# Embedding interactions with a small network on one core: one comparison per chunk, shorter VectorE subtractions, pair loads right behind stores

## What is computed

```python
e = jnp.stack([tbl_0[ids[:, 0]], ..., tbl_25[ids[:, 25]]], axis=1)
combined = jnp.concatenate([dense_features[:, None, :], sparse_features], axis=1)
interactions = jnp.einsum('bfd,bgd->bfg', combined, combined)
interactions_flat = interactions[:, _IU0, _IU1]
z = jnp.concatenate([dense_features, interactions_flat], axis=1)
h = jnp.concatenate([z, r_dense_features], axis=1)
h = jnp.maximum(h @ W_top1 + b_top1, 0.0)     # 607 x 512
h = jnp.maximum(h @ W_top2 + b_top2, 0.0)     # 512 x 256
y = h @ W_top3
```

## Time and profile before

| | |
|---|---|
| Time, median of 3 runs | 526.63 us (525.46 to 535.25) |
| The profiled execution's own time | 522.24 us |
| Its span | 520.4 us |
| TensorE, busy | 373.9 us (72%) |
| GpSimd, busy | 352.1 us (68%) |
| VectorE, busy | 257.9 us (50%) |
| ScalarE, busy | 205.5 us (39%) |
| TensorE's granted clock, mean | 0.852 of full speed |
| DMA queues, share of 16 engines | 34.3% (SP's), 12.6% (the gathers) |

### The profile page before, as it was taken

How to read it: one execution, slowest core, us unless ns; L and a number is a source line. 1 busy time by engine, 2 the same in 40 slices (tenths; PEclk the granted TensorE clock), 3 DMA queues, 4 the chain that set the end, 5 groups by cost and what they waited for, 6 DMA issues and landing times.

```text
span 520.4 us, 8177 instructions
## 1 busy us (share of the span) xinstructions
PE 373.9 (72%) x3360; PEld 299.5 (58%) x3360; DVE 257.9 (50%) x186; ACT 205.5 (39%) x278; POOL 352.1 (68%) x266
## 2 busy tenths in 40 slices
PE   0969689496908450899975782889981937669997
PEld 0758477475807340778854471678851726456887
DVE  5778689483965105659760535649760001102123
ACT  2996945424623123153622425154530314225500
POOL 7888888887888775868887676868887570730000
PEclk9988989797968775799997795799995866779999
DMA  8975746961763513358357353358331520114320
GB/s 197 250 180 153 198 114 182 295 176 42 193 161 108 147 50 90 86 153 210 99 144 193 91 134 95 86 136 219 102 84 50 150 67 6 51 32 108 73 65 10
DMA packets 40327, 64.85 MB, mean 125 GB/s; under 512 B 22013, under 2 KB 22909, under 8 KB 40292
## 3 DMA queue, kind: packets, MB, share of 16 engines
q1 hardware_dynamic: 31152, 47.14, 34.3%
q0 software_dynamic: 8192, 16.79, 12.6%
q10 hardware_dynamic: 948, 0.41, 0.3%
HBM read 54.08 MB, written 10.23 MB: 124 GB/s over the span
## 4 chain that ended last, share of the span: by engine, by line
PE 38%; POOL 24%; issue 15%; another core or an unknown queue 12%; DVE 9%; DMA 1%; ACT 1%; DVEq 0%; ACTq 0%
POOL rows L571 24%; PE look_bank L610 12%; PE short_bank L693 9%; PE out_bank L640 7%; DVE one_hot L901 5%; PE out_bank L654 4%; PE out_bank L649 3%; PE short_bank L678 3%; DVE low_table L888 2%; PE out_bank L666 1%; DMA rows<-in_tbl,all_ids 1%; DVE low_pairs L946 1%; DMA all_ids<-in_ids 0%; DVE low_dense L946 0%
## 5 line engine op out<-in xcount | busy, mean ns | idle before, releaser
L571 POOL DMA_INDIRECT rows<-in_tbl,all_ids x256 | 351.1, 1371 | 109.4 <-issue 75.7
L901 DVE TENSOR_TENSOR one_hot<-spread_ids,chunk_row 128x2048 fp32r<-128x2048 int32 (+2 forms) x82 | 171.2, 2123 | 49.2 <-PE look_bank L610 22.3
L610 PE MATMUL look_bank<-one_hot,high_table 125*128 125x512 f32 x328 | 148.5, 453 | 22.3 <-DVE low_table L888 12.0
L610 PE MATMUL look_bank<-one_hot,low_table 125*128 125x512 f32 x328 | 139.4, 425 | 4.5 <-issue 4.5
L914 DVE COPY all_combined<-short_bank 128x512 f32<-128x512 f32 x32 | 21.7, 690 | 163.9 <-PE short_bank L678 73.3
L610 PEld LDWEIGHTS look_bank<-one_hot,high_table 125*128 125x128 f32 x328 | 69.4, 212 | 44.3 <-DVE low_table L888 12.0
L693 PE MATMUL short_bank<-all_combined 128*59 128x54 f32 x2048 | 71.5, 228 | 23.9 <-issue 22.3
L693 PEld LDWEIGHTS short_bank<-all_combined 128*59 128x59 f32 x2048 | 65.8, 142 | 34.5 <-issue 33.8
L610 PEld LDWEIGHTS look_bank<-one_hot,low_table 125*128 125x128 f32 x328 | 69.1, 211 | 21.8 <-issue 7.5
L678 PE MATMUL short_bank<-identity,rows 128*128 128x128 f32 x256 | 40.0, 303 | 57.8 <-issue 30.1
L678 PEld LDWEIGHTS short_bank<-identity,rows 128*128 128x128 f32 x256 | 31.2, 154 | 63.1 <-issue 57.2
(11 more groups left out here) (41 smaller groups left out, 200.8 us busy)
## 6 DMA issues: line engine op xcount, KB each, us to landing
whole_table<-in_tbl SPq DMA_DIRECT2D x36, 448.0 KB
spread_ids<-in_ids_by_feature SPq DMA_DIRECT2D x40, 256.0 KB
block_scratch<-all_dots SPq DMA_DIRECT2D x24, 208.0 KB
rows<-in_tbl,all_ids POOLq DMA_INDIRECT x256
block_scratch<-all_dots SPq DMA_DIRECT2D x24, 104.0 KB
whole_table<-in_tbl SPq DMA_DIRECT2D x4, 560.0 KB
pairs<-block_scratch SPq DMA_DIRECT2D x72, 29.2 KB
whole_table<-in_tbl SPq DMA_DIRECT2D x36, 52.0 KB
```

The lines of the kernel that those rows point to most:

```text
L571: nc.gpsimd.indirect_dma_start(rows[:, t % 2, slot, :], None, tables[ROW_FEATURES[slot]][:, :], bass.IndirectOffsetOnAxis(ap=all_ids[:, t, ...
L610: last = nc.tensor.matmul(look_bank[s % LOOK_BANKS][:], table_parts[part][s % TABLE_PLACES][0:ROWS_K, c, :], one_hot[0:ROWS_K, (chunks_bef ...
L901: last = nc.vector.tensor_tensor(one_hot[:, place:place + n, :], spread_ids[:, s % ID_PLACES:s % ID_PLACES + 1, :].to_broadcast([P, n, COLS]),
```

## The change

Three edits. (1) VectorE makes the one-hots with one comparison of 512 columns per chunk; and the low parts of tables (in two instructions, of 512 or 640 columns), pairs and weights (one instruction per slice of 512) are subtracted in shorter instructions. Since the lists of views are shared, ScalarE's casts of pairs and weights are cut in the same way; its casts of tables aren't. (2) At a block's end SP issues the pair loads right behind the stores, ahead of the first look's ids and table instead of behind them. (3) Behind a block's four tiles stand 4, 6, 7 and 7 products of the block before instead of 6 each. No sum and no number type changes.

```diff
--- before.py
+++ after.py
@@ -78,6 +78,8 @@
 
 HALVES_AFTER = [6, 5, 5, 4]
 
+OUTS_AFTER = [4, 6, 7, 7]
+
 FIRST_MOVES = [(0, 8), (8, N_LOOK)]
 
 PART_PAIRS = [(HIGH, HIGH), (HIGH, LOW), (LOW, HIGH)]
@@ -169,7 +171,7 @@
                 half[4:-1] + one[:2] + half[-1:] + one[2:-1] + two[:2] + one[-1:] + two[2:]][u]
     first = (m + 1) * 2 * N_LOOK + sum(HALVES_AFTER[:u])
     looks = [step for half in range(first, first + HALVES_AFTER[u]) for step in look_steps(half)]
-    outs = out_steps(m - 1)[6 * u:6 * u + 6] if m > 0 else []
+    outs = out_steps(m - 1)[sum(OUTS_AFTER[:u]):sum(OUTS_AFTER[:u + 1])] if m > 0 else []
     if u == 0:
 
         return looks[:2 * SPLIT_BESIDE] + merge(looks[2 * SPLIT_BESIDE:], outs, 1.0)
@@ -417,12 +419,12 @@
 
         def weight_parts(w):
 
-            return w[:, 0, :], w[0:K_PAIRS, 1:K_TILES, :]
+            return [w[:, 0, :]] + [w[0:K_PAIRS, k, :] for k in range(1, K_TILES)]
 
         def input_views(m):
 
             return [(dense_cols[:, m % 2, :], high_dense[:], low_dense[:, m % 2, :]),
-                    (pairs[0:K_PAIRS], high_pairs[0:K_PAIRS], low_pairs[0:K_PAIRS])]
+                    *[(pairs[0:K_PAIRS, k], high_pairs[0:K_PAIRS, k], low_pairs[0:K_PAIRS, k]) for k in range(PAIR_SLICES)]]
 
         def scratch_of(h):
             return block_scratch[h % 2] if h < 2 * LAST else last_scratch[h - 2 * LAST]
@@ -544,12 +546,10 @@
                 for h in ends:
 
                     store_part(h, range(IN_QUAD // 2) if last else range(IN_QUAD))
-                for s in looks[:1]:
-                    load_ahead(s)
                 for h in ends:
                     if h % 2 == 1 or h >= 2 * LAST:
                         load_part(h, range(IN_QUAD // 2) if last else range(IN_QUAD))
-                for s in looks[1:]:
+                for s in looks:
                     load_ahead(s)
                 if u == PER_BLOCK - 2 and m < LAST:
 
@@ -885,8 +885,11 @@
                 i, c = s % TABLE_PLACES, CHUNKS[s % N_LOOK]
 
                 dve.wait_ge(table_high, s + 1)
-                nc.vector.tensor_tensor(low_table[i][0:ROWS_K, 0:c, :], whole_table[i][0:ROWS_K, 0:c, :],
-                                        high_table[i][0:ROWS_K, 0:c, :], ALU.subtract).then_inc(table_split, 1)
+                for part in halves(s):
+                    a, b = part[0], part[-1] + 1
+                    last = nc.vector.tensor_tensor(low_table[i][0:ROWS_K, a:b, :], whole_table[i][0:ROWS_K, a:b, :],
+                                                   high_table[i][0:ROWS_K, a:b, :], ALU.subtract)
+                last.then_inc(table_split, 1)
 
             def make_half(half):
 
@@ -897,10 +900,10 @@
                 if free_places(half):
 
                     dve.wait_ge(half_done, free_places(half))
-                for c, n, place in runs_of(s, h):
+                for c in halves(s)[h]:
                     last = nc.vector.tensor_tensor(
-                        one_hot[:, place:place + n, :], spread_ids[:, s % ID_PLACES:s % ID_PLACES + 1, :].to_broadcast([P, n, COLS]),
-                        chunk_row[c_all][:, c:c + n].unsqueeze(2).to_broadcast([P, n, COLS]), ALU.is_equal)
+                        one_hot[:, (chunks_before(s) + c) % HOT_PLACES, :], spread_ids[:, s % ID_PLACES, :],
+                        chunk_row[c_all][:, c:c + 1].to_broadcast([P, COLS]), ALU.is_equal)
                 last.then_inc(one_hot_ready, 1)
                 if h == 1 or by_act(half + 1):
                     split_table(s)
```

## The result

The changed kernel takes 572.7 us (median of 4 runs, 571.9 to 577.5) against 526.05 (4 runs, 524.3 to 535.3) for the kernel before: ratio 1.0892, 95% interval 1.0802 to 1.0983. It is slower; 472 was forecast, with a range up to 528. The profiled execution took 571.9, its span is 569.7.

What follows compares the result with a forecast made beforehand. The prediction found no single engine bounding the whole kernel, with gathers slowed by VectorE and holds on TensorE. 522.2 + 3 + 1 - 20 - 38 = 468 us, plus 4.4 for the runs' median, gave 472, range 440 to 528.

Steps and rivals of the forecast that it cites:

- Shorter VectorE instructions: VectorE does 18.4 us more work, mostly off the path: +3 us in the start and +1 us behind it.
- The gathers: GpSimd's gathers wait less for VectorE's shorter instructions, ending TensorE's waits for rows in the first block: -20 us (8 to 26).
- No gather over 1.6 us: Predicted sign in the changed kernel's table by batches, beside batches of 20 to 25 us next to a busy VectorE.
- The holds: TensorE's late-seen results, in steps of some 8.4 us over full-rate batches, end sooner with shorter batches: -38 us (10 to 55).
- rival 3: Gathers at full rate hold TensorE, and long VectorE instructions now shield it: 552 us, chance 0.12.
- Pair loads and products: Pair loads behind stores: 0 us (-3 if a table stalls, +8 if causing a hold); respread products: 0 (-2, +3).
- The sum: Whole kernel: 522.2 + 3 + 1 - 20 - 38 = 468 us profiled, forecast as 472 for the runs' median.
- The rule on SBUF: Skill rule: tensor_tensor with two SBUF inputs contends only with GpSimd's reads, so shorter instructions give gathers nothing; the prediction disagreed.
- Slower: Outcome that the whole changed kernel is slower than before by over 2%, chance 0.12.

Runs made afterwards that it cites:

- e1: Kernel before with only the comparisons cut to one per chunk of 512 columns, on a chip without holds: 418.1 us, 0.884 of the kernel before.
- e4: Kernel before with only the moved pair loads and the new spread of product steps, on a chip without holds: 475.4 us, ratio 1.004.
- e8: Changed kernel with one waited-for GpSimd memset of 256 columns behind each gather, on a chip with holds: 482.5 us, 0.921 of the kernel before.
- e5: Changed kernel itself, run again on a second chip, one with holds: 572.2 us, 1.096 of the kernel before.
- e11: Changed kernel with gathers of 64 columns per sample in place of 128 (half the bytes), on a chip with holds: 561.4 us, 1.073 of the kernel before.
- e13: Changed kernel itself, run again on a third chip, one without holds: 436.6 us, 0.925 of the kernel before.
- e16: Changed kernel with GpSimd starting a batch after the freeing tile's dots, not its turn, on a chip with holds: 557.7 us, 1.061 of the kernel before.
- e6: Kernel before with only one comparison per chunk, as in e1, on a second chip, one with holds: 549.3 us, 1.046 of the kernel before.
- e17: Kernel before with one comparison per chunk and batches started after dots instead of turns, on a chip with holds: 541.0 us, 1.029 of the kernel before.

## Why the prediction was wrong

**Shorter VectorE instructions: right.** There are 303 comparisons, 685 ns in the median, and 457 VectorE instructions in place of 186. That their price stays off the path was right as well: e1 is 55 us faster with 221 more of them.

**The gathers: right, and under-sized where it can be seen.** Their waits fell by 70.9 us (351.1 to 280.2), and most take 0.94 us. The term was -20, bounded by the 23.6 us of waits for rows behind the start. On a chip without holds these waits are 70.6 us in all (e4), and the gain there was 36 to 55 us. On the chip of the trace it was hidden behind what follows. "No gather over 1.6 us" was wrong: 18.96, 8.38, 4.78 and 1.70 us. I had written of the traced gathers that they never wait for the instruction behind the present one. That held for nearly all gathers before and after, but not for these.

**The holds: this is the step that failed, with its sign.** I took -38 us (10 to 55), on the ground that a hold lies over a batch and ends with it, so shorter batches make shorter holds. By the table above holds cost 54 us before and 136 after: +82. The observation was right and the inference from it wrong. A hold is what a batch at full rate does; the long VectorE instructions that made gathers wait were what kept tiles smooth, and the change took this cover away (the same gathers with pauses in their place are 90 us faster, e8 against e5). Rows 2 had it: the two batches without waits are the ones in which TensorE worked 7 and 10 of 19.9 us. I priced this as rival 3 (552 us) and gave it 0.12. Against it I held nine gathers at full rate from 95.9 to 106.0 without a step of 8.4 us; but holds need a backlog, and what they stop is short matmuls and the news of finished work, and nine gathers prove little on either. Even so 552 was low: I counted four tiles of 31 us, and eleven of the 16 tiles have dots of over 5 us, up to 40, where six had, up to 16.

**Pair loads and products: right where it was measured.** Forecast 0 and 0; e4 measured +0.4%, on a chip without holds and beside the long comparisons. Beside short ones they weren't taken apart: the whole change is 23 us slower than the comparison alone on the chip with holds.

**The sum on either kind of chip.** Without the holds' term it was 526.6 - 16 = 511, or 0.97. Chips without holds gave 0.925 for the whole change. On those with holds the 82 us above come on top, -36 + 82 = +46; as the 82 come from the same four medians, this splits the measured 46.7 and doesn't check it.

**The rule on SBUF.** By the section "Who interferes with whom" of the Trainium skill's page "SBUF — State Buffer" shorter `tensor_tensor` instructions would leave the gathers as they were. The section calls its reason inferred, and these runs disagree with it once more: 1371 to 1094 ns with shorter instructions, and 18.96 us where a gather began with a comparison.

**The chances.** Slower had 0.12, and the range ended at 528. One trace of one chip couldn't show that holds differ between chips, but it showed that the two halves of my argument, long instructions slow the gathers and full-rate batches stop TensorE, worked against each other. This asked for more than 0.12.

## What to carry to other kernels

When a change frees an engine, look in the trace of before for the stretches in which that engine already runs freely, and read what the others get done there: that is how the whole kernel will look afterwards. Gathers that GpSimd issues at their full rate can cost more on TensorE than they save on GpSimd; a short GpSimd instruction behind every second gather took the changed kernel from 572 to 500 us on chips with holds and lost nothing on one without (437 to 426). And time a change on more than one chip before believing it: this one was 0.925 of the time on one chip and 1.096 on another, with intervals of 0.5% and 1.2% to either side.

## What the runs showed of the hardware that I had not expected

- On three of the six chips, and in the first measurement, gathers 1.25 us apart cut TensorE's short matmuls down to between none and three per gather, most often one, and delay the news of finished matmuls by up to some 20 us, and this fades as they stand further apart (idle time by issue 104.5 us at 1.25, 4.4 at 2.3). On the other three, gathers 1.25 us apart do neither (dots 3.68 us). The bytes hardly count (561 us with half of them in e11, 572 in e5).
- It doesn't look like the loading of instructions in large blocks. The page's part on DMA queues has, for the changed kernel,

```profile
q8 instruction: 26, 0.43, 0.3%
```

  26 packets of 16,384 bytes, while the dots alone stood still 87 times, and none of the 26 starts between 180.4 and 207.4 us, the time of the hold shown above. The Trainium skill's page "Runtime: NRT & Kernel Launch", section "Instruction fetch mechanics", says that instructions are refilled in blocks of 16 KiB, 256 instructions; the packets agree with it in size, and 26 times 256 is nearly TensorE's 6720 instructions.
- A gather can be starved while VectorE's instructions with two SBUF inputs follow each other without a pause: 18.96 us in the changed kernel, 18.13 to 18.95 in e5, e11, e13 and e16, 18.75 in e6 and e17, each time a gather that started in the first or second comparison behind two copies from PSUM, and until VectorE came to its next copy from PSUM or fell idle (the end lies 0.8 to 0.9 us behind the start of the one or the beginning of the other). A shorter case, 4.76 us in e8, began further behind the copies. Most gathers that start near a seam wait nothing; what tells them apart stays open.
